# An expert layer in two phases: the first layer's rows stored to the output, all pair results added in four rounds, five early tiles of each phase

## The reference, cut to what matters

```
x = x + xattn(layernorm(x), token_ids, ctx)      # layer 1: 4 experts, chosen by token id
x = x + ffn(layernorm(x), G, gate, up, down, lora_A, lora_B)   # layer 2: 8 experts, top 2 by router
# xattn: out = (silu(h @ ctx[e].T) * (h @ ctx[e].T)) @ ctx[e].T for the token's expert e
# ffn:   scores = softmax(x @ G); the 2 best experts e1, e2 with weights w1, w2
#        out = sum_k w_k * (down[e_k] @ (silu(gate[e_k] @ x) * (up[e_k] @ x)) + lora_B[e_k] @ lora_A[e_k] @ x)
```

## Time and profile before

| | |
|---|---|
| median of 3 runs | 313.19 us |
| the profiled execution | 313.26 us, of which the span is 311.5 us |
| PE busy | 266.6 us (86%) |
| DVE, ACT, POOL busy | 236.1, 149.6, 168.6 us |
| mean granted TensorE clock | 0.925 of full speed |

### The profile page before, as it was taken

One profiled execution on the slowest core, in us unless ns is written; L12 is line 12 of the kernel. 1 busy time (PEld: TensorE's weight loads), 2 busy tenths in 40 slices (PEclk: granted clock), 3 DMA queues, 4 the chain that ended last, 5 costly groups with the idle time before them and its releaser, 6 DMA issues. The chain is left out here.

```text
span 311.5 us, 6118 instructions
## 1 busy us (share of the span) xinstructions
PE 266.6 (86%) x1629; PEld 230.0 (74%) x1629; DVE 236.1 (76%) x726; ACT 149.6 (48%) x350; POOL 168.6 (54%) x173
## 2 busy tenths in 40 slices
PE   0568999999999999999599949859999999999910
PEld 0546787888888887888488839748999899999700
DVE  8686848779987998799838985888999986666600
ACT  4532433444444445435324433226666678888810
POOL 3659425443488638863672181427544427867760
PEclk9958999999999999999789995679999999999965
DMA  7562999611043114410333035259977756999830
GB/s 272 198 207 76 337 241 333 233 34 38 0 157 103 36 34 170 162 43 2 136 137 102 2 136 170 80 149 313 303 245 208 216 176 92 208 247 151 106 51 0
DMA packets 23280, 45.98 MB, mean 148 GB/s; under 512 B 4540, under 2 KB 8636, under 8 KB 22656
## 3 DMA queue, kind: packets, MB, share of 16 engines
q0 software_dynamic: 9488, 21.84, 25.9%
q1 hardware_dynamic: 13760, 23.74, 25.2%
HBM read 24.49 MB, written 25.80 MB: 161 GB/s over the span
## 5 line engine op out<-in xcount | busy, mean ns | idle before, releaser
L399 POOL DMA_INDIRECT out<-pair_out,dest_now x38 | 49.8, 1311 | 32.5 <-DVE pair_out L924 13.4
L475 ACT ACTIVATE aT_hi<-p_aT 128x512 fp32r<-128x512 f32 x19 | 11.4, 600 | 55.3 <-PE p_aT L1038 55.3
L1112 PE MATMUL p_y<-ctx_hi,aT_hi 128*128 x76 | 32.6, 429 | 0.3 <-ACT aT_hi L475 0.3
L1112 PE MATMUL p_h<-ctx_hi,xT_hi 128*128 x72 | 29.9, 416 | 1.4 <-ACT xT_hi L471 1.4
L350 POOL DMA_INDIRECT xin<-x,gather_row x19 | 20.3, 1070 | 19.7 <-DVE rec L725 15.6
L1113 PE MATMUL p_y<-ctx_lo,aT_hi 128*128 x76 | 30.9, 406 | 0.0
L372 POOL DMA_INDIRECT rows_a<-rec,dest x19 | 18.9, 996 | 21.8 <-DVE dest L799 17.1
L1113 PE MATMUL p_h<-ctx_lo,xT_hi 128*128 x72 | 28.4, 395 | 0.0
L357 POOL TENSOR_TENSOR rstd<-var_eps,neg_half 128x1 f32<-128x1 f32 x19 | 12.7, 670 | 26.8 <-DVE var_eps L694 24.0
L1058 PEld LDWEIGHTS p_rt<-route_w,x2T 128*128 128x128 f32 x152 | 20.5, 198 | 3.9 <-issue 2.5
L486 ACT ACTIVATE rec<-rec,neg_mean 128x512 f32<-128x512 f32 x19 | 13.7, 723 | 18.3 <-DVE var_eps L734 17.4
(11 more groups left out here) (254 smaller groups left out, 792.7 us busy)
## 6 DMA issues: line engine op xcount, KB each, us to landing
whole<-ctx_t SPq DMA_DIRECT2D x4, 1024.0 KB, 6.7
pair_x_late<-rows_b SPq DMA_DIRECT2D x14, 258.0 KB, 4.3
pair_x_early<-rows_a SPq DMA_DIRECT2D x12, 258.0 KB, 3.2
pair_x_late<-rows_a SPq DMA_DIRECT2D x10, 258.0 KB, 3.7
whole<-w_up SPq DMA_DIRECT2D x4, 576.0 KB, 6.3
rows_a<-pair_x_early SPq DMA_DIRECT2D x8, 258.0 KB, 11.8
rows_b<-pair_x_early SPq DMA_DIRECT2D x8, 258.0 KB, 12.6
pair_x_early<-rows_b SPq DMA_DIRECT2D x8, 258.0 KB, 3.2
```

The source lines that it names most:

```text
L399: nc.gpsimd.indirect_dma_start(out=out, out_offset=bass.IndirectOffsetOnAxis(ap=rows, axis=0), in_=pair_out[:, s % ORING, :], in_offset=No ...
L1112: nc.tensor.matmul(to, hi(i), w_hi(i), start=(i == 0), stop=False)
```

## The change

The changed kernel keeps the products and moves the rest:

- `keep(t)`, new: POOL stores the centred record of each of the 19 tiles to `out`, at the token's own row (`own_row`, one more operation on DVE).
- All 44 pair results are evicted by ACT and added to `out` by accumulating DMAs; `pair_finish` and `pair_done` are gone. Phase 0 adds the mean back. There are four rounds (`ROUNDS`: pairs 0 to 4, 5 to 9, 10 to 26, 27 to 43), and a round begins when all stores of the one before have landed.
- One early list for both phases, after tile 13: five tiles of phase 0 and five of phase 1 are early. It is computed in the last step of layer 1. The order of pairs is then phase 0 early, phase 1 early, phase 0 rest, phase 1 rest.
- The batches end at 4, 8, 11, 14 and 19 (before 4, 8, 12, 15, 19). `pair_gates` of the batches 0 to 2 runs one step after `places`, the scatters of the batches 0 to 2 one step later. The power for the second deviation is taken once for a batch. Ring `rec` has 11 slots: tiles 0 to 7 use 0 to 7 and tiles 8 to 18 use 0 to 10.
- The whole lists are cut in three parts with pair iterations between them, and the last batch's gates and places stand behind more pair work. A load of the whole lists waits until the turn of the pair 8 before it is done (`AHEAD`).

```
-XRING, RRING = 6, 8
-ARING, ORING = 14, 10
-BATCHES = [(0, 4), (4, 8), (8, 12), (12, 15), (15, 19)]
+XRING, RRING = 6, 11
+ARING, ORING, AHEAD = 14, 10, 9
+BATCHES = [(0, 4), (4, 8), (8, 11), (11, 14), (14, 19)]
+WRAP = 8
...
+ROUNDS = [0, EARLY, 2 * EARLY, 2 * EARLY + REST]
...
-            return t % RRING if t < LAST0 else t - LAST0
+            return t if t < WRAP else t - WRAP
...
             sp.wait_ge(filled, 2 * 16 * (NB + 1))
+            sp.wait_ge(lists_ready, 1)
+            wait_scattered(0, BATCHES[EARLY_BATCH][1])
+            for s in range(EARLY):
+                load_pair(s)
+            wait_scattered(1, BATCHES[EARLY_BATCH][1])
             sp.wait_ge(y_ready, STEPS)
+            for s in range(EARLY, 2 * EARLY):
+                load_pair(s)
+            sp.wait_ge(lists_ready, 2)
+            wait_scattered(0, STEPS)
+            for s in range(2 * EARLY, PAIRS):
+                if s == ROUNDS[3]:
+                    wait_scattered(1, STEPS)
+                sp.wait_ge(tx_ready, s - AHEAD + 1)
                 load_pair(s)
...
+            def keep(t):
+                pool.wait_ge(xc_ready, t + 1)
...
+                nc.gpsimd.indirect_dma_start(
+                    out=out, out_offset=bass.IndirectOffsetOnAxis(ap=own_row[:, t:t + 1], axis=0),
+                    in_=record(t), in_offset=None, bounds_check=TOKENS - 1, oob_is_err=False,
+                ).then_inc(kept[rec_slot(t)], 16)
...
             def store(s):
+                pool.wait_ge(evicted, s + 1)
+                if s == 0 or s == 2 * EARLY:
+                    for i in range(RRING):
+                        pool.wait_ge(kept[i], 16 * rec_users(i, STEPS if s else BATCHES[EARLY_BATCH][1]))
+                if s in ROUNDS[1:]:
                     for i in range(ORING):
+                        pool.wait_ge(stored[i], 16 * ((s - i + ORING - 1) // ORING))
...
-                    compute_op=ALU.bypass if s < PHASE else ALU.add,
+                    compute_op=ALU.add,
...
+            keep(STEPS - 2)
+            inverse_deviation2(len(BATCHES) - 1)
+            keep(STEPS - 1)
             for s in range(3):
                 store(s)
-            for t in range(*BATCHES[-1]):
-                scatter(t, 1)
+            for t in range(last0, STEPS):
+                scatter(t, 0)
             for s in range(3, PAIRS):
                 store(s)
+                if s < 3 + STEPS - last0:
+                    scatter(last0 + s - 3, 1)
...
-                if k == BATCHES[EARLY_BATCH[0]][1] + 3:
-                    early_list(0)
+                if k == BATCHES[EARLY_BATCH][1] + 4:
+                    early_lists()
...
+            lo2(3)
+            combine(2)
+            al2(1)
+            gate_up(2)
+            lo2(4)
             pair_gates(last)
-            pair_finish(0)
+            pair_iteration(3)
             places(last)
-            al2(1)
-            combine(2)
-            gate_up(2)
-            lo2(3)
-            whole_lists()
-            lo2(4)
-            for i in range(3, PAIRS + 2):
+            list_tiles()
+            pair_iteration(4)
+            list_steps()
+            pair_iteration(5)
+            list_rows()
+            for i in range(6, PAIRS + 2):
                 pair_iteration(i)
```

More of the change, by code:

```diff
@@ L369, in scatter @@
                 pool.wait_ge(dest_ready, b + 1)
+                pool.wait_ge(gates_ready, b + 1)
                 pool.wait_ge(stats_put, b + 1)
-                rows, cols, done = ((rows_a, slice(0, ROW), scattered_a), (rows_b, slice(META, REC), scattered_b))[phase]
+                rows, cols, done = ((rows_a, slice(0, ROW), scattered_a), (rows_b, slice(META, REC), scattered_b))[m]
                 nc.gpsimd.indirect_dma_start(
-                    out=rows, out_offset=bass.IndirectOffsetOnAxis(ap=dest[:, t, phase:phase + 1], axis=0),
+                    out=rows, out_offset=bass.IndirectOffsetOnAxis(ap=dest[:, t, m:m + 1], axis=0),
                     in_=rec[:, rec_slot(t), cols], in_offset=None, bounds_check=XROWS - 1, oob_is_err=False,
@@ L421, in _ @@
                 split_ctx(E1 - 1, half, ctx_lo_ready)
+            SCATTER_AT = {BATCHES[0]: 5, BATCHES[1]: 5, BATCHES[2]: 5, BATCHES[3]: 4}
             def scatters(k):
-                for b, (t0, t1) in enumerate(BATCHES[:-2]):
-                    if t1 + 4 <= k < t1 + 6:
-                        half = k - t1 - 4
-                        for t in range(t0 + 2 * half, t0 + 2 * half + 2):
-                            scatter(t, 0)
-                            scatter(t, 1)
+                for (t0, t1), behind in SCATTER_AT.items():
+                    if k == t1 + behind:
+                        some = range(t0, t0 + 2) if t1 + behind < STEPS - 1 else range(t0, t1)
+                    elif k == t1 + behind + 1:
+                        some = range(t0 + 2, t1)
+                    else:
+                        continue
+                    for m in range(2):
+                        for t in some:
+                            scatter(t, m)
             for k in range(STEPS):
@@ L837, in whole_lists @@
-            def whole_lists():
+                dve.wait_ge(total_ready, 1)
+                count = counts_of(EARLY_BATCH)
+                each, some = [P, NB, TILES], [P, 2, EARLY, NB]
+                for m in range(2):
+                    last = nc.vector.tensor_tensor(reached[:, m], count[:, m].unsqueeze(2).broadcast_to(each),
+                                                   full_from[:].unsqueeze(1).broadcast_to(each), ALU.is_ge)
+                step(last, do)
+                step(nc.vector.tensor_reduce(n_tiles[:], reached[:], AX_X, ALU.add), do)
@@ L876, in whole_lists @@
-                nc.vector.tensor_scalar(pair_expert[:, PHASE:PAIRS], at_expert[:, 1, :], 1.0, float(E2 - 1), ALU.add,
+                for m in range(2):
+                    last = nc.vector.scalar_tensor_tensor(pair_row[:, m, EARLY:PHASE], at_row[:, m, :], taken_row[:, m, :],
+                                                          at_limit[:, m, :], ALU.add, ALU.min)
+                step(last, do)
+                nc.vector.tensor_copy(pair_expert[:, 0, EARLY:PHASE], at_expert[:, 0, :])
+                nc.vector.tensor_scalar(pair_expert[:, 1, EARLY:PHASE], at_expert[:, 1, :], 1.0, float(E2 - 1), ALU.add,
@@ L981, in _ @@
             lo_act(STEPS - 1)
-            places(last - 1)
             lo2(0)
-            early_list(1)
             choose(STEPS - 3)
@@ L1253, in _ @@
             route(STEPS - 2)
[L1254 removed]
             tx(2)
             ta(0)
+            turn_x2(STEPS - 1)
+            down(0)
             route(STEPS - 1)
             up(1)
[L1259 removed]
+            tx(3)
+            up(2)
+            ta(1)
+            tx(4)
+            pair_iteration(3)
             total(len(BATCHES) - 1)
             rank(len(BATCHES) - 1)
[L1262 to L1266 removed]
+            for i in range(4, PAIRS + 2):
                 pair_iteration(i)
```

310 lines of the change are left out of this document (139 added, 171 removed).

## The result

The changed kernel takes 328.21 us (median of 4 runs, 328.12 to 329.38) against 313.03 us: ratio 1.0494, 95% interval 1.0449 to 1.0539. It is slower by 15.2 us; I had forecast 316.2 with a range of 307.5 to 322.0. The profiled execution took 328.19 us with a span of 326.4 us, so the sum is made against that one: +14.9 us to the 313.26 of before.

What follows compares the result with a forecast made beforehand. It took PE to bound the layer 1 steps and the pairs. Early list -6.5, ring +2.2, step 18 +0.3, `own_row` +0.3 and later `dest` (203.8 for 196.54, less 0.3) gave +3.3, some 316.5, rounded to 316.2 us; range 307.5 to 322.

Steps and rivals of the forecast that it cites:

- slower: Whole kernel: more than 1% slower than before, above 316.3 us, chance 0.46.
- the ring distance: Layer 1, tiles 8 and 12: later scatters make residuals wait for ring slots, +4.0 us, net +2.2 with batch work spread.
- the path from `dest` to the last store: After the last `dest`: later `tx(10)`, four fewer iterations to go, lower clock after a PE stop; net 0.
- The early list leaves the step: Layer 1, step 15: without the early list the step falls from 14.26 to 7.72 us, -6.5 us.
- the 1.8 us I wanted back from spread batch work: Layer 1: DVE's batch work, spread over more steps, gives back 1.8 of the 2.1 us it cost.
- +5 if both land late: Layer 1: upper bound of the net cost if the scatters for tiles 8 and 12 both land late, +5 us.
- The keeps: The 19 `keep` DMAs on POOL: they fit in its idle time and DVE hardly delays them, 0 us.
- The handover: Layer 1 to pairs: PE idles 3.7 us, residual +1.8, more pair work 6.0; `dest` at 203.8 instead of 196.54.
- What stands is D: After layer 1: with the part behind it net 0, only the time of the last `dest`, called D, counts.
- 2.0 (the clock): At `tx(10)`: PE idles there for 4 us, which again brings the lower clock, +2.0 us.
- Stores that add in all rounds: Pair phases: ACT evicts and adding stores throughout keep 2.2 us for a pair, 0 us.
- POOL and the DMAs become the bound: Pair phases, a rival: adding stores and round changes with landings of 7 us cost +5, 321 us, chance 0.12.

Runs made afterwards that it cites:

- e4: Kernel before with its first early list made in step 16 instead of step 15: 310.7 us, ratio 0.9935.
- e1: Changed kernel with all 11 slots of the record ring in use from the first tile on: 322.36 us, ratio 1.0089.
- e7: Changed kernel with the last batch's gates and places ahead of pair iterations 2 and 3, rank and exponentials moved too: 328.51 us, ratio 1.0515.
- e2: Changed kernel with phase 1 results in a table of their own and no wait between rounds, phases not summed: 326.55 us, ratio 1.0205.
- f2: Changed kernel with the edits of e1, e2 and e7, last `rows_b` scatters at round changes, last `rows_a` scatters ahead of stores 0 to 2: 321.55 us, ratio 1.0066.
- e3: Changed kernel with the last tile's second product ahead of `tx(0)` on PE: 333.49 us, ratio 1.0422.
- f1: The same kernel as e3, run once more: 329.80 us, ratio 1.0349.
- after_third: Changed kernel as it is, on a chip where the kernel before takes 319 to 320 us: 330.27 us, ratio 1.0357.
- before_again: Kernel before as it is, nothing changed, on a chip where it takes 319 to 320 us: 319.86 us, ratio 1.0012.

## Why the prediction was wrong

The direction was right (slower had the largest chance, 0.46) and the time was not: +14.9 where my sum had +3.3. Two steps of the sum failed: the ring distance was mis-sized, and the path from `dest` to the last store had its wait and its period wrong. Point by point:

1. **The early list leaves the step: -6.5.** Right: 14.26 to 8.35, -5.9, no stop of over 0.4 us there. e4 shows that the gain is not free: to where the list goes, part of the stop goes along.
2. **Ring distance: +4.0 forecast, +8.4 measured. This step failed in size.** The mechanism was as put: the third scatter of the batch started at 98.43 (I had 97.5), landed 2.9 us later, and the residual at 101.38 waited for it. Of the 0.9 us, 0.4 are the power for four columns, 1.01 us and not 0.6; the rest is that the power ahead of it started at 94.02 and not at 93.45, while PE came to its turn 0.6 us sooner than before (100.66 for 101.24). So the stop was 3.4 us and not 2.0, and what stood behind it at a mean clock of 0.87 added 1.8, which I had left to the range. The second step was worse, 3.2 for 1.3 (5.1 and 5.0 in the two later traces). Of the 1.8 us I wanted back from spread batch work, 0.4 came. Net it is +8.0, and without the 1.8 for the clock still more than my bound "+5 if both land late"; e1 gives 8.6 us back.
3. **The keeps: 0.** They took 972 to 1082 ns each on POOL, as rows 7 had let expect, and none of PE's stops waits for one; no run leaves them out. The cost that I did not look at is the other direction, DVE held by POOL (below).
4. **The handover: `dest` at +7.3.** Nearly right: +8.4, with PE's stop before `tx(0)` 3.88 (forecast 3.7), and residual to `dest` 19.4 (my terms 13.5 and 6.0, less 0.7 for `pair_finish`, give 18.8, and `dest` at 203.6, not the 203.8 of the text). e7 shows that the last 4 us of that delay did not matter: `store(2)` waits for ACT's third evict, and that came no sooner when `dest` did (23.7 us behind the last residual for 24.1). "What stands is D" was therefore wrong as a path, and the next point counts from a place that is not on it.
5. **`dest` to the last store: 0 forecast, +5.4 measured. The second step that failed.** Up to the last scatter it is as forecast (11.94 us behind `dest` for 11.6). Then the load took 5.0 us and not 2.7, beside two adding stores and the other scatters, at a DMA share of 1.01 (222.24 to 227.22) where it was 0.52 before (205.43 to 208.14): `tx(10)` at `dest` + 20.6 for 18.4. And the 33 periods took 78.7 us and not 72.6. The first of them, behind the stop, took 3.9 and not 2.2, for which the sum had 2.0 (the clock); another 3.9 lie between the turns 23 and 27, where the load of pair 24 came late.
6. **Stores that add in all rounds: 0, failed with 5.** The period is 2.2 only while loads come in time. The round changes took 8.2, 8.1 and 5.75 us. "POOL and the DMAs become the bound", which I gave 0.12 and +5 with landings at 7 us, came true in part, beside the ring and not instead of my forecast: the landings of 6.2 us cost time, but over PE's loads, and e2 prices the rounds at 2.5 to 4.9 us. The price of the landing stood in the trace of before, 5.9 us over 264 to 280 at a DMA share of 1.07, and I had taken 3.1.

The rivals were written as if only one could come true, and the range ended at 322 because none of its cases held both failed steps. That their prices (8.6 from e1, 2.5 to 4.9 from e2) add is not shown: no run has just these two edits, and f2, which has both and three more, takes off 9.3 us in all (1.0357 to 1.0066), hardly more than e1. What the handover costs by itself is open too, since e3 and f1 do not test it.

The Trainium skill's page "SBUF — State Buffer", section "Who interferes with whom", also says that a DVE instruction with two SBUF inputs waits for a GpSimd instruction that reads SBUF. The trace agrees: small operations of two operands (3 to 32 elements) took 0.97 to 1.38 us in the kernel before and 1.17 to 2.02 in the changed one where they met POOL's subtraction, 0.16 to 0.24 elsewhere. In e4 it hit the list itself:

```profile
151.84 1.97 DVE L813 TENSOR_TENSOR left<-n_tiles,taken 128x7 f32<-128x7 f32 x1
```

```profile
151.94 0.59 POOL L362 TENSOR_TENSOR rstd<-var_eps,neg_half 128x1 f32<-128x1 f32 x1
152.49 1.28 POOL L385 TENSOR_TENSOR down_lo<-whole,down_hi 80x512 fp32r<-80x512 f32 x1
```

## What to carry to other kernels

Delaying the release of a buffer cost nothing here until the ring came round, and then it cost the stop (3.41 us at 104.07) and in the longer one the lower clock behind it (0.87): count the ring's slots against the step in which the slot is read, and use every slot from the first tile on. Where a kernel waits for landings between rounds, take the landing time from rows with the same DMA share and the same kind of store as after the change, not from the quiet place where the old wait stood (here 5.9 us and not 3.1). And where two rivals have separate causes, give the case in which both come true a chance and a price.

## What the hardware showed

- An accumulating store from POOL holds it for 1.54 us (plain 0.97) and is apart from the next by 1.85; it lands 6.2 us after issue over 250 to 280 us, at a DMA share of 0.97 (5.9 in the kernel before, at 1.07).
- A batched power on POOL is not one price: 0.58 us for 128x1, 1.01 for 128x4.
- A DVE operation that took 0.22 us started while POOL issued a DMA directly ahead of its subtraction and did not end until that subtraction had (1.96 us, e1). It is not the DMA alone that holds: in the changed kernel 53 small two-operand operations of DVE started during a DMA issue of POOL, and 50 of them took 0.16 to 0.39 us (0.21 and 0.18 at 159.61 and 159.74). The three that were held started in the last 0.14 to 0.58 us ahead of a subtraction that stood directly behind the DMA. What holds an operation that starts first in the profile is not shown.
- On three chips one or two operations of ScalarE start late with a releaser outside the core: `aT_hi` 3.6 us later behind the last turn than on A (after_third), `up_b` 6 us (before_again). On these chips the kernel before takes 2% more and the changed one 0.6%, so ratios of one chip do not carry to another.
